# The attention mix of four heads issued in two halves, two heads at a time

## The reference: what is computed

```
# layer 1, self attention "l1a_": 16 heads of 16 features, rotary, causal
# layer 3, cross attention "l3x_": 32 heads of 8 features; keys and values from ctx (4 x 256 x 128)
logits = einsum('bqhd,bkhd->bhqk', q, k) * scale
w      = softmax(logits)                      # over the 256 keys (causal mask in l1a_)
attn   = einsum('bhqk,bkhd->bqhd', w, v)
out    = attn @ Wout
```

## Time and profile before

| | |
|---|---|
| median of three runs | 1608.46 us |
| the profiled execution, its own time | 1609.24 us |
| its span in the profile | 1607.4 us |
| PE busy (share of the span) | 1131.6 us (70%) |
| DVE busy | 1060.7 us (66%) |
| ACT busy | 496.2 us (31%) |
| POOL busy | 575.2 us (36%) |

### The profile page before, as it was taken

One profiled execution on the slowest core, in us unless ns is written; L12 is line 12 of the kernel. 1 busy time (PEld: TensorE's weight loads), 2 busy tenths in 40 slices (PEclk: granted clock), 3 DMA queues, 4 the chain that ended last, 5 costly groups with the idle time before them and its releaser, 6 DMA issues. The chain is left out here.

```text
span 1607.4 us, 21391 instructions
## 1 busy us (share of the span) xinstructions
PE 1131.6 (70%) x6058; PEld 713.9 (44%) x6058; DVE 1060.7 (66%) x1795; ACT 496.2 (31%) x957; POOL 575.2 (36%) x596
## 2 busy tenths in 40 slices
PE   7535547999309695555898896698938788766970
PEld 3212135777105573112465544576724334445860
DVE  6999975873695557998886783410345778745454
ACT  3423322333402252332211302233303346622430
POOL 0046613552655113662000042033431532204746
PEclk9669977999759798998998999799978869986995
DMA  5064347996321403432400162323420140048944
GB/s 190 31 252 144 126 132 223 300 322 240 99 71 30 129 4 131 154 133 105 148 1 0 60 147 30 116 73 115 152 79 1 40 120 4 3 141 232 333 143 121
DMA packets 139682, 195.87 MB, mean 122 GB/s; under 512 B 35632, under 2 KB 99138, under 8 KB 138316
## 3 DMA queue, kind: packets, MB, share of 16 engines
q1 hardware_dynamic: 96636, 144.80, 28.6%
q0 software_dynamic: 12704, 29.36, 6.3%
q10 hardware_dynamic: 30256, 20.65, 4.5%
HBM read 142.80 MB, written 31.72 MB: 109 GB/s over the span
## 5 line engine op out<-in xcount | busy, mean ns | idle before, releaser
L165 POOL TENSOR_SCALAR rstd<-moments 128x4 f32<-128x4 f32 x24 | 6.5, 270 | 402.0 <-DVE moments L148 402.0
L177 PE MATMUL psum<-w_ident,h 128*128 128x128 f32 x144 | 29.5, 386 | 111.3 <-DVE h L155 111.3
L558 PE MATMUL psum<-l1s_read,w_ident 128*128 128x512 f32 x128 | 66.0, 641 | 52.6 <-DVE l1s_read L623 52.6
L558 PE MATMUL psum<-l0s_read,w_ident 128*128 128x512 f32 x128 | 65.1, 634 | 52.6 <-DVE l0s_read L623 52.6
L1906 DVE TENSOR_REDUCE l3x_neg<-psum 128x2 f32<-128x512 f32 x128 | 80.7, 683 | 23.8 <-PE psum L1777 23.8
L1881 ACT ACTIVATE l3x_work<-psum 128x512 f32<-128x512 f32 x128 | 72.5, 598 | 50.9 <-PE psum L1800 50.6
L546 POOL TENSOR_TENSOR l1s_drive<-l1s_du,l1s_bc 128x1024 f32<-128x1024 f32 x32 | 75.3, 2354 | 35.2 <-DVE psum L619 35.2
L546 POOL TENSOR_TENSOR l0s_drive<-l0s_du,l0s_bc 128x1024 f32<-128x1024 f32 x32 | 75.2, 2351 | 35.3 <-DVE psum L619 35.3
L1162 PE MATMUL psum<-l0f_w_in,l0f_xT 128*128 (+1 forms) x224 | 77.3, 468 | 0.1
L177 PEld LDWEIGHTS psum<-w_ident,h 128*128 128x128 f32 x144 | 25.1, 200 | 117.8 <-DVE h L155 115.5
L1037 POOL DMA_INDIRECT l3f_x<-l3f_h_rows,l3f_token_of x64 | 59.3, 927 | 50.3 <-DVE l3f_token_of L1433 28.8
(11 more groups left out here) (641 smaller groups left out, 3160.7 us busy)
## 6 DMA issues: line engine op xcount, KB each, us to landing
l0f_w_in<-in_l0f_w_in SPq DMA_DIRECT2D x56, 352.0 KB
l0s_bc<-l0s_scratch SPq DMA_DIRECT2D x16, 1024.0 KB, 5.2
l1s_bc<-l1s_scratch SPq DMA_DIRECT2D x16, 1024.0 KB, 5.2
l3f_w_in<-in_l3f_w_in SPq DMA_DIRECT2D x32, 384.0 KB
l0f_w_down<-in_l0f_w_down SPq DMA_DIRECT2D x56, 176.0 KB
l2f_w_in<-in_l2f_w_in SPq DMA_DIRECT2D x24, 352.0 KB
l0f_y_rows<-l0f_y ACTq DMA_DIRECT2D x56, 128.0 KB
l3f_w_down<-in_l3f_w_down SPq DMA_DIRECT2D x32, 192.0 KB
```

Of the source, the lines that this page charges most:

```text
L177: ins = nc.tensor.transpose(m.psum[:, at:at + P], m.h[:, t, k * P:(k + 1) * P], m.ident[:])
L558: ins = nc.tensor.matmul(m.pair(2 + c)[:, cols], lhsT=m.ident[:], rhs=rhs[:, cols], start=start, stop=stop, skip_group_check=True)
```

## The change: the mix in two halves

`mix` takes a second argument, `half`. Half 0 holds the heads 0 and 1 of the quad and is issued at step 4 * quad + 20; half 1 holds the heads 2 and 3 and is issued at step 4 * quad + 22, where the whole mix was. Half 0 waits for the exponentials of the first two heads of the quad and, from quad 2 on, for the bank to be free; half 1 waits for all four exponentials, and its last matmul alone tells ACT that the bank is filled. Number, shape and operands of the matmuls stay as they are, and so does all that the other engines do.

```
-        def mix(quad):
-            pe.wait_ge(self.exp_done, (quad + 1) * self.QUAD)
-            if quad >= 2:
+        def mix(quad, half):
+            pe.wait_ge(self.exp_done, quad * self.QUAD + 2 * half + 2)
+            if quad >= 2 and half == 0:
                 pe.wait_ge(self.mixed_ready, quad - 1)
             out = self.bank(6 + quad % 2)
-            for j in range(self.QUAD):
+            for j in range(2 * half, 2 * half + 2):
                 for kt in range(2):
...
-            ins.then_inc(self.mixed_filled, 1)
+            if half:
+                ins.then_inc(self.mixed_filled, 1)
...
             for s in range(s0, s0 + step):
-                if s % 4 == 2 and 0 <= (s - 22) // 4 < n // self.QUAD:
-                    mix((s - 22) // 4)
+                if s % 2 == 0 and 0 <= (s - 20) // 4 < n // self.QUAD:
+                    mix((s - 20) // 4, s % 4 // 2)
```

## The result

The changed kernel takes 1619.04 us in the median of its first five runs, against 1607.88 for the kernel before beside it: a ratio of 1.0073, interval 1.0048 to 1.0097. A second set gave 1.0060 (1.0035 to 1.0085). By the ratios it is slower by 10 to 12 us (the medians of the second set, 1617.28 and 1609.22, differ by 8.1); I had forecast +12.9 us, 1621.4.

What follows compares the result with a forecast made beforehand. TensorE alone was taken to bound l1a_'s main stretch, while in l3x_ no engine was full and they took turns. Adding +7.7 us (l1a_) and +5.2 (l3x_) to 1608.46 gave 1621.4 us; 8-in-10 range 1611 to 1633.

Steps and rivals of the forecast that it cites:

- A half lasts as long as a whole mix: Mixes of both attentions: two heads still need four rounds, so a half costs 0.90 us in l1a_, 1.13 in l3x_.
- The code's order of passes: Mixes: by the cited rule thirteen rounds, a split costing 0.47 us, total about 1602; the trace's four rounds spoke against it.
- Rival 1: Mixes: a half has half the rounds, total 1599.5, or passes go in code order, about 1602; 8% together.
- l3x_, 7.37 us for eight heads and no waits: Steady l3x_: eight heads take 7.37 us against 7.13, PE's waits filled; +2.9 us, and +0.4 for "outT".
- rival 2: Both attentions: the 2.3 us of waits per eight heads stay beside the added work, total 1648; 8%.
- l3x_, start: +0.8: Start of l3x_ at 1.2 GHz: one half finds only a 0.9 us wait to lie in; +0.8 us net.
- l3x_, tail: +1.1: Tail of l3x_: halves partly covered by PE's 3.0 us of idling there; +1.1 us.
- l1a_, the hole: +0.3, and the clock: -1.5: l1a_: three halves add 2.70 us against the 2.44 us load wait; the clock behind it returns to 1.00.
- l1a_, eight halves in the full stretch: +7.2 - 0.3: l1a_, steps 32 to 60, where PE is full: eight halves of 0.90 us, less 0.3 for waits for ACT's copy.
- l1a_, tail: +2.0: l1a_, steps 64 to 80: five halves of 0.90 us less 1.98 us of PE idling, taken as +2.0 us.
- Total: Whole kernel: +7.7 us in l1a_ and +5.2 in l3x_, +12.9 in all, giving 1621.4 us, slower by 0.8%.
- Rival 3: l1a_ or l3x_: two-wide rounds get a stretch or two granted clock 0.50, total 1624 to 1632 us; 10%.

Runs made afterwards that it cites:

- adjacent: Against the kernel before: in both attentions the mix is issued as two halves, one right behind the other at the whole mix's step; ratio 1.0015.
- start_l3x: Against the kernel before: halves only for quads 0 to 2 of l3x_, later quads and l1a_ whole; ratio 0.9994.
- steady_l3x: Against the kernel before: quads 0 to 3 of l3x_ whole, halves from quad 4 on, l1a_ whole; ratio 1.0034.
- l3x_only: Against the kernel before: halves in l3x_ only, whole mixes in l1a_; ratio 1.0030.

## Why the prediction was right, point by point

- *A half lasts as long as a whole mix.* Right, and shown three ways: eight passes in four rounds of two in the trace, the one-head blocks of 0.84 us, and the return to one block when nothing lies between. 1.00 + 0.11 us in l3x_ for the 1.13 used.
- *The code's order of passes.* The rule of the Trainium skill that I weighed ("TensorE: Matmul & The Clock Gate", Part 3, "The mechanism", packed matmuls start in program order) is again not what the traces show: in `adjacent` the passes of heads 2 and 3, issued by a second call, run beside those of heads 0 and 1, sixteen passes in 1.02 us. In the mix of the earlier trace rows all eight passes of 256 columns start (578.41 to 578.69) before the first of 128 columns (578.87), though in the code head 0's 128 columns stand ahead of head 1's 256. Rival 1 is out in both its forms: a half takes 1.00 us to the next scores, and no mix takes thirteen rounds.
- *l3x_, 7.37 us for eight heads and no waits.* Measured 7.38, without a wait of PE. +0.25 each, for +0.24. From head 32 to the last maximum that makes +4.1 in all, where I had 2.9 + 0.4 = +3.3: the three groups of eight with "outT" in them take 8.08 for 7.73, and up to three others take 7.5 to 7.9 for 7.13, the one from head 40 with a wait of 0.18 us for the load of the negated maxima, which I had not counted; my +0.4 was too small for both. This was worked out from releases that came as little as 0.2 us early, and rival 2, that the waits stay, is out.
- *l3x_, start: +0.8.* Wrong by 4 us, in sign too. The term took the half-clock stretch of the earlier trace rows as given, though in l1a_ I had let the same kind of work bring the clock back. Here the clock did come back with it: -3.3, and -3.2 in start_l3x.
- *l3x_, tail: +1.1.* Measured 1.23 - 0.82 = +0.4.
- *l1a_, the hole: +0.3, and the clock: -1.5.* Measured -0.1 to head 32, and from there to head 36 -0.66 with one half in it, so about -1.5 for the clock. That the halves bring it is likely and not shown: 1.00 behind the hole in all five kernels with halves or quarters there, 0.50 in six of the seven others, 1.00 in one.
- *l1a_, eight halves in the full stretch: +7.2 - 0.3.* Measured from head 36 to head 60, six halves, +4.47, that is 0.74 each and 5.9 for eight. The price of a half is right (0.93 in the trace, less 0.06); what it covers at "out" was 0.25 and not 0.1 in every second quad. In the kernel before the "out" at 574.41 starts 0.24 us after the matmul ahead of it and lasts 0.49 us to the next; in the changed kernel the same is 0.06 and 0.44.
- *l1a_, tail: +2.0.* From head 63 on +1.34.
- *Total.* Forecast +7.7 and +5.2. The stretches measure +5.7 (+6.3, +5.2) and +1.2 (+1.5, +1.7): 6.9 to 7.8 in place of 12.9, and the step that failed is the start of l3x_. The runs say +10 to +12 us by the ratios, +8.1 by the medians of the second set, so all but the last is more than the two stretches hold. Outside them the span is 1389.2 us before and 1392.0 and 1388.4 in the changed kernel, and 1384.3 to 1395.0 over all twelve profiles, so the +2.9 of the first profile says nothing; steady_l3x and l3x_only have ratios of about +5 us with stretches of +4.7 and +1.7. Whether a part of it is lasting (profiles of one execution each can't tell 3 us in the remaining 1400) stays open. So the total came closer to the forecast than its terms: the mechanism and the price of a half were right, the closeness of 1621.4 to 1619.04 is in part luck.
- Rival 3, a lower clock, did not come: PEclk is 1.00 throughout both steady parts. The two-wide rounds cost no clock here.

## What to carry to other kernels

In these traces matmuls with weights of 32 columns ran side by side only as far as nothing of another shape stood between them in TensorE's order; a block was as long as the work of its fullest column group (four passes each: 0.84, 0.85 and 0.88 us with one, two and four groups filled). Cut such a block across the work of each group (here by keys), not between the groups (by heads). When a re-ordering both covers waits and adds work, write out TensorE's sum for one period with and without the waits (here, in eight heads of l3x_, 2.26 + 0.3 us of work came and the 2.3 us of waits went): if the added work is as large as the waits that go, a re-ordering gains nothing, and another cut of the same work may.

## What the runs showed that I had not expected

- Passes from two separate calls, with a semaphore wait between, share the array as if issued together (sixteen passes in 1.02 us in `adjacent`). So do halves of different quads: at the end of l3x_ in the changed kernel the last three halves meet with nothing between. The timeline merges their 24 passes; in cuts, at 1420.20 to 1420.30 and at 1421.46 to 1421.50, four start together (half 1 of quad 30 with half 0 of quad 31), and the last half, which fills two groups, starts alone at 1421.45:

```profile
1420.21 2.30 PE L1823 MATMUL psum<-l3x_work,l3x_v 128*32 128x256 f32 x24
...
1420.21 0.44 PE L1823 MATMUL psum<-l3x_work,l3x_v 128*32 128x256 f32 x4
...
1421.45 0.42 PE L1823 MATMUL psum<-l3x_work,l3x_v 128*32 128x256 f32 x2
```

- A little more TensorE work at the start of a stage made the stage faster: the kernels with the first quads of l3x_ in halves had lost 0.7 to 2.2 us by head 24 and were 3.2 to 3.3 us ahead by head 32, with the clock at 1.00.
- The clock after the hole in l1a_ was 1.00 once without more work. What a single profile shows of the clock behind a wait may be the luck of that execution.
